# Attention of a macaron block on one core: key tiles in groups of three, each maxima's matmul ahead of its score, score banks in plain rotation

## The reference

```python
x = x + 0.5 * ffn(layernorm(x))         # hidden 2048, weights replaced by their signs, relu, scales
x = x + attention(layernorm(x))         # 16 heads of 32, softmax(q k^T / sqrt(32)) v, then w_o
x = x + 0.5 * ffn(layernorm(x))
```

```python
scores = einsum('bhqd,bhkd->bhqk', q, k) * SCALE
probs = softmax(scores, axis=-1)
attn = einsum('bhqk,bhkd->bhqd', probs, v)
```

## Time and profile before

| | us |
|---|---|
| median of 3 runs (lowest, highest) | 3001.04 (2997.48, 3006.79) |
| the profiled execution | 3000.77 |
| its span, first to last instruction | 2999.0 |
| TensorE busy | 2918.1 (97%) |
| VectorE busy | 2051.5 (68%) |
| ScalarE busy | 1610.4 (54%) |
| GpSimd busy | 1381.3 (46%) |

### The profile page before, as it was taken

The page is one execution under the profiler, slowest core; times in us unless marked ns, Lnnn a source line. Parts: engine busy times, 40 slices in busy tenths (PEclk is TensorE's granted clock), DMA queues, the critical chain, the costliest instruction groups (busy, mean ns, idle before and its releaser), DMA issues.

```text
span 2999.0 us, 38468 instructions
## 1 busy us (share of the span) xinstructions
PE 2918.1 (97%) x14528; PEld 1936.4 (65%) x14528; DVE 2051.5 (68%) x3050; ACT 1610.4 (54%) x2851; POOL 1381.3 (46%) x522
## 2 busy tenths in 40 slices
PE   6999998998999999999999999999999999999999
PEld 5888887887755555555555555555555448888887
DVE  5555555777778787878787878787878355555553
ACT  5444444332266666666666666666666554333333
POOL 0000000000089898988898888888888730000000
PEclk9999999999999999999999999999999989999999
DMA  4110112554398989898989898989898872222100
GB/s 154 57 57 28 29 30 79 189 195 167 131 221 188 228 197 227 198 230 194 225 199 228 198 229 195 224 200 225 199 228 197 225 209 71 56 57 57 57 29 29
DMA packets 189274, 459.97 MB, mean 153 GB/s; under 512 B 90272, under 2 KB 91296, under 8 KB 148768
## 3 DMA queue, kind: packets, MB, share of 16 engines
q0 software_dynamic: 36720, 267.40, 39.0%
q1 hardware_dynamic: 152368, 190.11, 22.2%
HBM read 121.91 MB, written 67.63 MB: 63 GB/s over the span
## 4 chain that ended last, share of the span: by engine, by line
PE 85%; ACT 8%; DVE 3%; DMA 1%; issue 1%; POOL 0%; ACTq 0%; SPq 0%; DVEq 0%; POOLq 0%
PE bank L951 16%; PE bank L511 15%; PE bank L530 15%; PE bank L920 15%; PE bank L924 11%; PE bank L642 7%; ACT att_p L908 7%; PE bank L382 3%; PE bank L975 1%; PE bank L967 1%; DMA att_dma_acc<-att_p 1%; DVE norm_inv L109 1%; ACT head_raw L286 0%; DVE norm_work L119 0%; PE bank L176 0%
## 5 line engine op out<-in xcount | busy, mean ns | idle before, releaser
L853 DVE TENSOR_REDUCE att_row_max<-bank 128x1 f32<-128x512 f32 x2048 | 1255.4, 682 | 343.7 <-PE bank L924 343.7
L908 ACT ACTIVATE att_p<-bank 128x512 f32<-128x512 f32 x2048 | 1042.3, 624 | 437.6 <-PE bank L920 431.3
L809 POOL TENSOR_TENSOR att_acc<-att_acc,att_p 128x2048 f32<-128x2048 f32 x217 | 1049.6, 4837 | 46.1 <-ACT att_p L908 41.4
L920 PE MATMUL bank<-att_q,att_k 98*128 98x512 f32 x2048 | 856.3, 420 | 25.9 <-ACT att_p L908 17.8
L924 PE MATMUL bank<-att_k,att_q 96*128 96x512 f32 x2048 | 808.8, 397 | 10.8 <-DVE att_row_max L853 10.3
L920 PEld LDWEIGHTS bank<-att_q,att_k 98*128 98x128 f32 x2048 | 385.8, 189 | 424.1 <-issue 209.1
L951 PE MATMUL bank<-att_p,att_v 128*32 128x512 f32 x4096 | 501.2, 607 | 0.0
L443 DVE TENSOR_TENSOR ffn_hid_lo<-ffn_hid,ffn_hid_hi 128x512 fp32r<-128x512 f32 x256 | 175.9, 688 | 418.5 <-ACT ffn_hid_hi L486 399.7
L483 ACT ACTIVATE ffn_hid<-bank,up_s 128x512 f32<-128x512 f32 x256 | 176.0, 688 | 483.8 <-PE bank L511 482.4
L924 PEld LDWEIGHTS bank<-att_k,att_q 96*128 96x128 f32 x2048 | 389.8, 190 | 62.3 <-DVE att_row_max L853 13.1
L511 PE MATMUL bank<-hi,ffn_up_w 128*128 128x512 f32 x1024 | 400.2, 391 | 10.7 <-DVE lo L123 10.7
(11 more groups left out here) (104 smaller groups left out, 2235.9 us busy)
## 6 DMA issues: line engine op xcount, KB each, us to landing
att_dma_acc<-att_p POOLq DMA_DIRECT2D x225, 1024.0 KB, 8.9
att_dma_acc<-att_dma_acc POOLq DMA_DIRECT2D x30, 1024.0 KB, 12.4
x<-x_after_ffn SPq DMA_DIRECT2D x16, 1024.0 KB, 7.4
att_q<-q_hi SPq DMA_DIRECT2D x64, 256.0 KB, 4.1
att_k<-k_hi SPq DMA_DIRECT2D x64, 256.0 KB, 10.6
x_after_ffn<-x_out SPq DMA_DIRECT2D x8, 1024.0 KB, 9.4
q_hi<-qkv_o_hi SPq DMA_DIRECT2D x32, 256.0 KB, 2.0
q_lo<-qkv_o_lo SPq DMA_DIRECT2D x32, 256.0 KB, 2.3
```

Source lines behind the costliest of these rows:

```text
L809: self.nc.gpsimd.tensor_tensor(self.acc[H % 2][:], a[:], self.prob[kt % PR][:], ALU.add).then_inc(self.summed, 1)
L853: self.nc.vector.tensor_reduce(self.row_max[odd][:, qt, q:q + 1], m[:], axis=AX.X, op=ALU.max).then_inc(self.m_read, 1)
L908: self.nc.scalar.activation(self.prob[kt % PR][:, q * CH:(q + 1) * CH], self.s_ps[S_BANK[kt * QC + q]][:], ACT.Exp, scale=SCALE).then_inc( ...
L920: self.nc.tensor.matmul(self.s_ps[S_BANK[i]][:], self.k_st[H % NB][0:KM, kt * P:(kt + 1) * P], self.q_st[H % NB][0:KM, q * CH:(q + 1) * CH ...
```

## The change

- `GROUPS` replaces `G` and `NG`: key tiles go in groups (0, 1, 2), (3, 4, 5), (6, 7, 8), (9, 10, 11), (12, 13), (14, 15). The last head keeps eight pairs (`PAIRS`).
- Within a unit the maxima's matmul, with its wait, is issued ahead of the score.
- The score banks go in plain rotation over all heads, (64 H + unit) mod 3; each score waits for the exponential three units back. `bank_order` is gone.
- The transposition moves from group 6 (tiles 12, 13), ahead of the output matmuls, to group 3 (tiles 9 to 11), behind them. On VectorE the negation and the two copies go together ahead of key tile 12. The slot moves with it.
- The sums stand behind the output matmuls of group 2 (tiles 6 to 8). ScalarE copies them ahead of tile 9, and the last output behind the second unit of tile 3.
- The interleaving in head 30 is written for a last group of any size; with two tiles it is what it was.

```diff
--- before.py
+++ after.py
@@ -649,43 +649,31 @@
             st.norm.tensor(pe, self.PE_AT[t], N + 1)
 
 
-def bank_order(units, banks, second):
-
-    ages, bank = list(range(banks)), []
-    for i in range(units):
-        b = ages.pop(1 if i in second else 0)
-        ages.append(b)
-        bank.append(b)
-    assert ages == list(range(banks))
-    last = {b: u - units for u, b in enumerate(bank)}
-    freed = []
-    for i, b in enumerate(bank):
-        freed.append(last[b] + 1)
-        last[b] = i
-    return bank, freed
-
-
 NB = 3
 KQ, KM = 3 * HD, 3 * HD + 2
-LEAD, G = 4, 2
-NG = KT // G
+LEAD = 4
+GROUPS = ((0, 1, 2), (3, 4, 5), (6, 7, 8), (9, 10, 11), (12, 13), (14, 15))
+PAIRS = tuple((kt, kt + 1) for kt in range(0, KT, 2))
+SUMS_GROUP, TURN_GROUP = 2, 3
 PR = 8
 SR, MR = 3, 4
 UNITS = KT * QC
-S_BANK, S_FREED = bank_order(UNITS, SR, (23, 46))
 AHEAD = LEAD * QC
-SUMS_AFTER = 3
-SUMS_AT, TURN_AT = QC * G * (SUMS_AFTER + 1), QC * 7 * G
+SUMS_AT, TURN_AT = QC * GROUPS[SUMS_GROUP + 1][0], QC * (KT - LEAD)
 SLOTS = UNITS + 2
 CHAINS = 2
 PER = 7 * 16
-TURN = KT - LEAD + 1
 NEG = 3
 
 
+def groups(H):
+
+    return GROUPS if H < NH - 1 else PAIRS
+
+
 def sums_after(H):
 
-    return SUMS_AFTER if H < NH - 1 else SUMS_AFTER - 1
+    return SUMS_GROUP if H < NH - 1 else 2
 
 
 def chains_joined(H):
@@ -874,14 +862,13 @@
 
     def vector_tile(self, dve, H, kt):
         T = H + 1 + (kt + LEAD) // KT
+        if kt == KT - LEAD and H + 1 < NH:
+            self.negate(dve, H + 1)
+            self.rows_out(dve, H + 1, self.turn_bank(H))
         for q in range(QC):
             p = QC * kt + q
             if T < NH:
                 self.reduce_block(dve, UNITS * (H + 1) + AHEAD + p, self.m_ps[m_bank(H, slot(p))], T % 2, (kt + LEAD) % KT, q)
-            if kt == TURN - 1 and q == 0 and H + 1 < NH:
-                self.negate(dve, H + 1)
-        if kt == TURN and H + 1 < NH:
-            self.rows_out(dve, H + 1, self.turn_bank(H))
         if H > 0 and kt == (14 if H < NH - 1 else 12):
             self.head_out.invert(dve, H - 1)
 
@@ -900,24 +887,24 @@
 
     def scalar_tile(self, act, H, kt):
         self.tile_free(act, H, kt)
-        if H > 0 and kt == G * (sums_after(H) + 1):
+        if H > 0 and kt == groups(H)[sums_after(H) + 1][0]:
             act.wait_ge(self.t_ready, H)
             self.head_out.copy_sums(act, H - 1, self.sums_bank(H - 1))
         for q in range(QC):
             act.wait_ge(self.s_ready, UNITS * H + QC * kt + q + 1)
-            self.nc.scalar.activation(self.prob[kt % PR][:, q * CH:(q + 1) * CH], self.s_ps[S_BANK[kt * QC + q]][:], ACT.Exp,
+            self.nc.scalar.activation(self.prob[kt % PR][:, q * CH:(q + 1) * CH], self.s_ps[(UNITS * H + kt * QC + q) % SR][:], ACT.Exp,
                                       scale=SCALE).then_inc(self.exp_done, 1)
-            if q == 1 and H > 0 and kt == G:
+            if q == 1 and H > 0 and kt == groups(H)[1][0]:
                 act.wait_ge(self.p_used, KT * H)
                 self.head_out.copy_out(act, H - 1, self.o_ps)
 
 
 
     def scores(self, pe, H, kt, q):
-        i = kt * QC + q
-        if UNITS * H + S_FREED[i] > 0:
-            pe.wait_ge(self.exp_done, UNITS * H + S_FREED[i])
-        self.nc.tensor.matmul(self.s_ps[S_BANK[i]][:], self.k_st[H % NB][0:KM, kt * P:(kt + 1) * P],
+        i = UNITS * H + kt * QC + q
+        if i >= SR:
+            pe.wait_ge(self.exp_done, i - SR + 1)
+        self.nc.tensor.matmul(self.s_ps[i % SR][:], self.k_st[H % NB][0:KM, kt * P:(kt + 1) * P],
                               self.q_st[H % NB][0:KM, q * CH:(q + 1) * CH], start=True, stop=True).then_inc(self.s_ready, 1)
 
     def maxima(self, m, T, qt, q):
@@ -995,26 +982,28 @@
         if u == 0:
             pe.wait_ge(self.neg_loaded, 32 * (H + 1))
             pe.wait_ge(self.ones_set, min(H + 1, NB))
-        for kt in range(G * u, G * u + G):
+        first = groups(H)[u][0]
+        for kt in groups(H)[u]:
             T = H + 1 + (kt + LEAD) // KT
             if kt == KT - LEAD and T < NH:
                 pe.wait_ge(self.loaded[T % NB], PER * (T // NB + 1))
             for q in range(QC):
-                self.scores(pe, H, kt, q)
                 if T < NH:
                     at = slot(QC * kt + q)
                     self.bank_free(pe, H, at)
                     self.maxima(self.m_ps[m_bank(H, at)], T, (kt + LEAD) % KT, q)
+                self.scores(pe, H, kt, q)
                 if beside:
-                    beside(QC * (kt - G * u) + q)
-        if G * u <= TURN < G * u + G and H + 1 < NH:
+                    beside(QC * (kt - first) + q)
+        if u > 0:
+            for kt in groups(H)[u - 1]:
+                self.out_tile(pe, H, kt)
+        elif H > 0:
+            for kt in groups(H - 1)[-1]:
+                self.out_tile(pe, H - 1, kt)
+        if u == TURN_GROUP and H + 1 < NH:
             self.bank_free(pe, H, TURN_SLOT)
             self.transpose_max(pe, H + 1, self.turn_bank(H))
-        for kt in range(G * u - G, G * u):
-            if kt >= 0:
-                self.out_tile(pe, H, kt)
-            elif H > 0:
-                self.out_tile(pe, H - 1, KT + kt)
         if u == sums_after(H) and H > 0:
             self.bank_free(pe, H, SUMS_SLOT)
             self.sums(pe, H - 1)
@@ -1027,6 +1016,7 @@
     for _t in range(NT):
         FIRST_FROM[_n, _t] = sum(k for at, k in FIRST_AT.items() if at < (_n, _t))
 FIRST_TURN = (NCH - 1, 6)
+FILL_FROM = QC * len(GROUPS[-1]) - 8
 FOUR_FROM = FIRST_FROM[NCH - 1, 0]
 
 
@@ -1346,24 +1336,25 @@
                 pe.wait_ge(qkv.qk_read, 8 * NCH)
                 pe.wait_ge(qkv.v_read, 4 * NCH)
                 for H in range(NH):
-                    for u in range(NG):
+                    for u in range(len(groups(H))):
                         def beside(i):
                             t = u + 1 if H == LAST else 0
-                            first = (H, u, i) == (LAST - 1, NG - 1, 0)
-                            if first:
+                            ahead = (H, u) == (LAST - 1, len(GROUPS) - 1) and i >= FILL_FROM
+                            if ahead and i == FILL_FROM:
                                 pe.wait_ge(att.m_read, UNITS * NH)
                                 pe.wait_ge(wo_done, 2)
                             if (H, u, i) == (LAST, 0, 0):
                                 pe.wait_ge(att.neg_dve, NEG * NH)
-                            if (H, u) == (LAST - 1, NG - 1) or (H == LAST and u < 3):
-                                oproj.product(pe, 0, t, range(STEPS * i // 8, STEPS * (i + 1) // 8))
+                            if ahead or (H == LAST and u < 3):
+                                j = i - FILL_FROM if ahead else i
+                                oproj.product(pe, 0, t, range(STEPS * j // 8, STEPS * (j + 1) // 8))
                             if (H, u, i) == (LAST, 3, 7):
                                 norm.tensor(pe, 0, 2 * NCH)
                             if (H, u, i) == (LAST, 5, 3):
                                 norm.tensor(pe, 1, 2 * NCH)
 
                         att.tensor_group(pe, H, u, beside)
-                for kt in range(KT - G, KT):
+                for kt in PAIRS[-1]:
                     att.out_tile(pe, LAST, kt)
                 att.sums(pe, LAST)
```

## The result

| | before | after |
|---|---|---|
| median of 4 (lowest, highest), us | 3001.81 (2997.48, 3006.79) | 3209.20 (3187.71, 3218.12) |
| ratio after / before, 95% interval | | 1.068 (1.063 to 1.073) |
| profiled execution; its span, us | 3000.77; 2999.0 | 3200.68; 3198.9 |
| TensorE busy, mean granted clock | 2918.1, 0.993 | 2972.9, 0.964 |

The forecast was 2982.6, with a range of 2967 to 2994. The profile of the changed kernel says where the time went: the chain of waits, and two groups of waits (engine, line, who waited for whom: us, times, longest).

What follows compares the result with a forecast made beforehand. TensorE was taken as the bound, on the chain of waits for 85% of the span. Thirty heads at -0.55 (-16.5), head 1 at -3.1 and head 30 at +1.4 give -18.2 from 3000.77: 2982.6 us, range 2967 to 2994.

Steps and rivals of the forecast that it cites:

- Moved later: First triple's output matmuls come 1.87 + 0.86 us later, and SyncE's queued loads with them; nothing seen to wait for these.
- Rival B: GpSimd and its DMA chains become the bound, their loop needing over 49.80 us as a mean: 3008 us; chance 0.06.
- Triples, VectorE's wait: In bursts of twelve, late maxima wait 0.34 us for VectorE: a triple takes 8.86, or 9.05 with the output copy.
- A: VectorE's wait in triples is far smaller, 8.62 us each in place of 8.86: 2961 us, 2970 at best; chance 0.15.
- D: VectorE's wait at the tenth to twelfth maxima of three triples is at its upper end, 0.73 us: 3019 us; chance 0.05.
- E: No tellable change: VectorE's wait 0.45 to 0.55, or head 30 at upper end, head 1 nothing: 2992 to 3000; chance 0.12.
- Rotation: Each score waits for the exponential three back, never two, saving 0.86 us per head.
- Order: Maxima ahead of scores within a unit: worth nothing by itself, but puts the later resource at the burst's front.
- Transposition: Behind its group's output matmuls, with VectorE's negation hidden; still taken at +0.30 us per head (ends 0.1 and 0.6).
- Heads 1 and 30: Extra terms: head 1 hides the stall from ScalarE's w_o rounding, -3.1 us; head 30, waiting for GpSimd, +1.4 us.
- The sum: Heads of 49.25 us, -0.55 each, -16.5 for 30; head 1 -3.1, head 30 +1.4: -18.2 in all, 2982.6 us.
- rival C: TensorE's clock falls in the triples, costing 1.58 us once per head: 3030 us; chance 0.02.

Runs made afterwards that it cites:

- e3: Kernel before, with SyncE's loads held until 14 scores of the head are made, nothing else changed: 3200.46 us, ratio 1.063-1.069.
- e4: Changed kernel, with GpSimd's join held until the last head's output tiles are used, when SyncE starts the loads: 2979.24 us, ratio 0.990-0.994.
- e12: Kernel before, with SyncE's loads held until 11 scores of the head are made: 3047.75 us, ratio 1.012-1.017.
- e13: Changed kernel, with only the first join (at head 1) held until the loads start: median 3014.30 us, executions from 2973.06 to 3174.97.
- e1: Changed kernel, with each v load on its own semaphore, awaited only ahead of a head's first output tile: 2980.70 us, ratio 0.991-0.995.
- e8: Changed kernel, with eight pairs again in every head instead of triples, all else kept: 2966.83 us, ratio 0.987-0.990.
- e5: Kernel before, with plain rotation of the score banks and nothing else: 2978.26 us, ratio 0.991-0.993.
- e7: Changed kernel, with v on its own semaphore and each score ahead of its maxima again: 2979.33 us, ratio 0.991-0.994.
- e6: Kernel before, with each maxima's matmul ahead of its score and nothing else: 2997.38 us, ratio 0.995-0.997.
- e9: Changed kernel, with v's load issued ahead of the q and k loads, all on one semaphore: 2976.02 us, ratio 0.989-0.992.

## Why the prediction was wrong

**The step that failed** is "Moved later": "Nothing that I can see waits for these: the loads are wanted in the fifth group, at 37." It put the delay at nothing, without a landing time. With the landing a constant behind the issue there would have been room: the loads started 6.0 us into a head and v landed 20.7 behind, so 2.7 more makes 29.4. The landing was no constant. v took 25.5 from its issue in place of 16.3 and was there at 41, because the delay let the join go out more than 1 us ahead of the loads (e3 and e4 show it from both sides, e12 the switch), and each wait for v kept it so (e13). The row that bore on it was at hand: the join's issue, which I read as a mark of GpSimd's loop and never set beside SyncE's first load, 0.2 us away. The delay was also mis-sized, 2.2 us and not 2.7, for the first triple ends with two output tiles; that would not have saved the forecast.

**Rival B** had the right neighbourhood ("the loads now start 2.7 us later, nearer to GpSimd's join") and the wrong direction and price: it asked what the loads do to the join's chain. The join did something to the loads. Its 3008 and the condition of a GpSimd loop over 49.80 aren't what happened; GpSimd was idle more than before (some 13 us of a head in place of 7).

**Triples, VectorE's wait**: right. Forecast 8.86, 9.05 with the copy; measured 8.85 and 9.06 (e1). So rivals A and D fall, and E as far as it rests on that wait. But the sum that the same part held, 8.86 for a triple against 8.70 for one and a half pairs, says that triples lose; I booked the whole as one gain with the rotation and never said so. e8 did.

**Rotation**: right, -0.86 (e5: 49.80 to 48.94).

**Order**: called worth nothing by itself. In triples so (e7), with pairs worth 0.30 a head (e6).

**Transposition**: taken at +0.30, measured +0.04. That is the whole difference between 49.25 forecast and 48.99 measured in e1.

**Heads 1 and 30**: in e1 head 1 takes 48.95 in place of 53.20, its stall gone; 4.25 less, where 3.65 were forecast. Head 30 takes 59.1 before, 57.2 in e1, 61.7 in e4 and 65.7 in e9. The forecast's +1.4 is smaller than these differ from each other, so no run here can judge it.

**The sum**: without the wait for v, 2980.70 against the 2982.6 forecast. That this is within 2 us is partly luck. Beside the kernel before on its own chip e1 gains 24.0 us, and e4 25.5, where 18.2 were forecast, and the transposition's 0.26 in 30 heads is 7.8 of that. So the arithmetic of TensorE's path was good to 6 or 7 us, and the queue that it moved cost 229.

**The clock** (rival C): the short waits for VectorE left it at its upper level, in e1 1.00 from 850 to 2300 us. In the change it was at 0.50 behind the wait shown, and the group behind that wait took 2.0 longer, which with the wait itself makes the 6.9 that this head lost.

## What to carry to other kernels

When a step moves, set each DMA issue that moves with it beside the issues of the other queues, and ask which now goes out first; a margin of about 1 us between two large groups of transfers is a finding, not a detail. A load on a shared semaphore is awaited by its earliest user: give the one that is needed a head later its own, or issue the one with short rows first. And compare a longer burst with the pace of the engine that drains it, per tile: here VectorE was slower than the burst, and longer bursts lost.

## What the runs showed of the hardware

- The same load of 256 KB in 128-byte rows took 3.3, 16.3 or 25.5 us to land, by what ran beside it (e9, before, after). Beside a moved tile its 128-byte packets passed one for one with packets of 8 KB, 98 in 4 us; without one, 1052 passed in 0.7 us (the change).
- A later start of one queue by 1.2 us moved the landing of its last load by up to 12 us more (e12). A program can stay in either mode for most of its heads: executions of one kernel took 2973 to 3175 us (e13).
- In the two heads shown SyncE's issue of a 256 KB load took 0.3 to 0.4 us until about 1.1 us behind the join's issue (before), and from 1.5 us behind it on 1.2 to 1.7, but for the first load (0.32) and v's (0.75) of the change.
- VectorE reads a 512-column bank each 0.60 us. Some nine weight loads in a head waited for it, 0.33 us on average and 0.8 at most, and TensorE's granted clock stayed at its upper level (e1, 950 to 2250 us).
- 4.7 us of idle brought TensorE's next 4 us to 0.50 (the change). Shorter idle stretches did so only at times: 1.39 us of it brought the next 4 us to 0.61 (e6, head 1), while behind 2.71 us they stayed at 1.00 (e12, at 1924).
